# Sending each row only to its two experts: routed blocks of 128 rows in place of all experts on all rows

## The reference

```python
x = layernorm(x + attention(x))            # 16 heads of size 8, softmax over 256 keys
scores = sigmoid(x @ gate_w.T)             # 8 experts
sel = top_k(scores + expert_bias, 2)       # two experts for each token
routed = x[tok] * score                    # the row is scaled, then for expert e of the row:
h = silu(routed @ w1[e].T) * (routed @ w3[e].T)
out_r = (h @ w2[e].T) * score
shared = silu(x @ sw1.T) * (x @ sw3.T) @ sw2.T
x = layernorm(x + shared + sum of the token's two out_r)
```

## Time and profile before

| | us |
|---|---|
| median of three runs | 844.6 |
| lowest and highest | 840.38, 847.2 |
| profiled execution, its time | 847.3 |
| profiled execution, its span | 845.5 |
| attention stage, to the last logits | 469 |
| expert stage | 376 |

### The profile page before, as it was taken

One profiled execution on the slowest core, in us unless ns is written; L12 is line 12 of the kernel. 1 busy time (PEld: TensorE's weight loads), 2 busy tenths in 40 slices (PEclk: granted clock), 3 DMA queues, 4 the chain that ended last, 5 costly groups with the idle time before them and its releaser, 6 DMA issues.

```text
span 845.5 us, 19602 instructions
## 1 busy us (share of the span) xinstructions
PE 762.4 (90%) x6228; PEld 472.6 (56%) x6228; DVE 708.3 (84%) x1430; ACT 579.6 (69%) x1192; POOL 472.3 (56%) x687
## 2 busy tenths in 40 slices
PE   2598999999999999999987889989999999999894
PEld 1234555555555555555545566666666666666662
DVE  5577999999999999999983688888888787887885
ACT  1038999998989999899884566555555655565551
POOL 3336654554555456455212466666766766666664
PEclk9998999999999999999998899999999999999997
DMA  5754767676777677676412633334444544444430
GB/s 156 161 121 105 168 170 168 148 167 169 164 155 178 149 165 167 171 161 144 103 34 68 172 91 91 107 99 104 119 119 110 124 124 124 124 124 121 116 86 26
DMA packets 201682, 109.36 MB, mean 129 GB/s; under 512 B 10496, under 2 KB 201088, under 8 KB 201600
## 3 DMA queue, kind: packets, MB, share of 16 engines
q1 hardware_dynamic: 200048, 105.88, 51.7%
q10 hardware_dynamic: 1552, 2.44, 1.0%
HBM read 73.94 MB, written 33.82 MB: 127 GB/s over the span
## 4 chain that ended last, share of the span: by engine, by line
PE 60%; DVE 11%; POOL 9%; issue 8%; DMA 7%; ACT 2%; SPq 1%; DVEq 1%; POOLq 0%; ACTq 0%
PE bank L732 15%; PE bank L704 10%; PE bank L717 7%; DMA probs<-route_dram 5%; PE bank L739 4%; PE bank L741 3%; PE bank L740 3%; DVE k_stack L1083 3%; POOL place L510 3%; POOL rstd L519 3%; PE bank L814 2%; PE bank L897 2%; PE bank L794 2%; PE bank L834 2%; PE bank L801 2%
## 5 line engine op out<-in xcount | busy, mean ns | idle before, releaser
L1009 DVE TENSOR_REDUCE negmax<-bank 128x2 f32<-128x512 f32 x512 | 320.3, 679 | 31.2 <-PE bank L717 28.7
L558 ACT ACTIVATE probs<-bank 128x512 f32<-128x512 f32 x512 | 291.4, 606 | 44.8 <-PE bank L704 41.1
L717 PE MATMUL bank<-k_stack,q_stack 48*128 48x256 bf16 x1024 | 164.2, 284 | 11.4 <-DMA k_stack<-k_parts_dram 7.3
L704 PE MATMUL bank<-q_stack,k_stack 50*128 50x256 bf16 x1024 | 158.0, 276 | 7.6 <-ACT probs L558 6.1
L739 PE MATMUL bank<-x_hi,hi_w 128*128 128x512 f32 x288 | 137.6, 478 | 14.8 <-DVE k_stack L1083 9.5
L732 PE MATMUL bank<-probs,v_aug 128*32 128x256 f32 x2048 | 139.4, 390 | 0.4 <-ACT attT L569 0.4
L1073 DVE TENSOR_TENSOR k_stack<-bank,probs 128x512 f32<-128x512 f32 x128 | 87.6, 684 | 49.1 <-DMA probs<-route_dram 31.5
L704 PEld LDWEIGHTS bank<-q_stack,k_stack 50*128 50x128 bf16 x1024 | 75.6, 95 | 92.5 <-ACT probs L558 48.5
L741 PE MATMUL bank<-x_lo,hi_w 128*128 128x512 f32 x288 | 114.4, 397 | 0.0
L740 PE MATMUL bank<-x_hi,lo_w 128*128 128x512 f32 x288 | 114.0, 396 | 0.0
L510 POOL TENSOR_TENSOR k_stack<-k_stack,probs 128x512 f32<-128x512 f32 x48 | 62.0, 1293 | 79.1 <-DVE k_stack L1083 71.3
(11 more groups left out here) (116 smaller groups left out, 1338.7 us busy)
## 6 DMA issues: line engine op xcount, KB each, us to landing
probs<-route_dram SPq DMA_DIRECT2D x128, 256.0 KB, 6.0
q_stack<-q_parts_dram SPq DMA_DIRECT2D x64, 192.0 KB, 3.7
k_stack<-k_parts_dram SPq DMA_DIRECT2D x64, 192.0 KB, 4.9
k_parts_dram<-k_parts SPq DMA_DIRECT2D x32, 192.0 KB, 2.2
q_parts_dram<-q_parts SPq DMA_DIRECT2D x32, 192.0 KB, 2.2
xT_sb<-xT SPq DMA_DIRECT2D x32, 128.0 KB, 2.2
k_parts_dram<-k_parts SPq DMA_DIRECT2D x32, 128.0 KB, 2.0
q_parts_dram<-q_parts SPq DMA_DIRECT2D x32, 128.0 KB, 2.2
```

The lines of the kernel that those rows point to most:

```text
L558: nc.scalar.activation(probs[h][:], score_ps[EXP_BANK[h]][:].rearrange("p (j t) -> p j t", j=NT), ACT.Exp).then_inc(exp_done, 1)
L704: mm = pe.matmul(score_ps[EXP_BANK[h]][:, j * T:(j + 1) * T], k_stack[b.ring][first:last, h // 2, j * P:(j + 1) * P], q_stack[b.ring][firs ...
L717: mm = pe.matmul(max_ps[MAX_BANK[h]][:, i * T:(i + 1) * T], q_stack[b.ring][first:last, h // 2, i * P:(i + 1) * P], k_stack[b.ring][first: ...
L1009: nc.vector.tensor_reduce(negmax[b.ring % 2][:, :, column], max_ps[MAX_BANK[h]][:].rearrange("p (i s) -> p i s", i=NT), AX_X, ALU.max, neg ...
```

## The change

The experts no longer see all rows. The 32 batches are cut into five chunks of 6, 8, 8, 6 and 4 batches (12, 16, 16, 12 and 8 tiles). Four slots after a chunk's last batch, DVE ranks its tokens in 26 short steps (`route_steps`, between the reductions of one slot): top two, a running count per expert, with two small matmuls on PE for the counts across partitions, and from that for every token and choice a row number in a DRAM table sorted by expert, each expert's part padded to whole blocks of 128. POOL then sends the rows with **indirect DMAs** (`scatter`), one for each tile and choice, 128 rows of 132 floats each (the row and its score): two or four at each of two places in a slot. Tables are first filled with zeros by 42 DMAs on ACT's queue, two at the start of each of 21 slots (`blanks`).

The expert stage runs over 42 "quads" of four blocks (168 blocks, 128 of them needed if nothing were padded). A quad is loaded by SP, transposed, and each block is multiplied in plain float32 with the weights of its own expert, whose column in SBUF is read into PE's registers from a table (`experts`, a load of four registers per quad). Silu takes the row's score as its scale, and the product takes it again; then a transpose, `down`, and the products go to DRAM. The **shared network** is computed apart, one group of 512 tokens in every two and a half steps, in three pieces in three successive steps. POOL **gathers** the two product rows of each token with 8 indirect DMAs per group, DVE adds them times the score (`combine`) at steps set by COMBINE_AT, and statistics follow a step later. The root of a whole chunk is one POOL instruction (`root`), and ACT does the last layernorm (`norm`). There are 52 steps, 0 to 51; quads end at 41. Gone are the x1T copy, the x1 copy in DRAM, the broadcast weights, the split of the down operand and `weigh`.

```diff
+        SHARED_AT = [1 + (5 * g) // 2 for g in range(GROUPS)]
+        COMBINE_AT = (12, 14, 16, 23, 25, 27, 29, 33, 35, 37, 39, 41, 43, 45, 47, 49)
+        LAST_STEP = COMBINE_AT[-1] + 3
...
+                pool.indirect_dma_start(c.rows_dram, bass.IndirectOffsetOnAxis(ap=slot_column(c, choice, i), axis=0),
+                                        x1_rows[:, c.t0 + i, :], None).then_inc(rows_out[c.c][choice], 16)
...
+            for g in range(GROUPS):
+                gather(g)
+                c = chunk_of_group(g)
+                if c.c and g == c.groups[0]:
+                    root(chunks[c.c - 1])
+            root(chunks[-1])
...
+            def root(c):
+                pool.wait_ge(eps2_set, c.c + 1)
+                tiles = slice(c.t0, c.t0 + c.n)
+                pool.tensor_tensor(rstd2[:, tiles], var_eps2[:, tiles], minus_half[:, 0:c.n], ALU.pow).then_inc(rstd2_set, 1)
...
+            def experts(k):
+                c = chunk_of_quad(k)
+                pe.wait_ge(route_step, steps(c, ROUTE_STEPS))
+                pe.load(registers[k % 2], expert_of[0:1, 4 * k:4 * k + 4])
...
+                for a in range(4):
+                    pe.matmul(up_ps[a // 2][:, a % 2 * 2 * C:a % 2 * 2 * C + 2 * C], xT_q[k % 2][:, a * P:(a + 1) * P],
+                              wall_up[:, bass.ds(first_column(k, a), 2 * C)], start=True, stop=True).then_inc(up_mm, 1)
...
+            def step(k):
+                if k + 1 < QUADS:
+                    rows_turned(k + 1)
+                if 0 < k <= QUADS:
+                    hidden_turned(k - 1)
+                if k < QUADS:
+                    experts(k)
+                    up(k)
+                if 0 < k <= QUADS:
+                    down(k - 1)
...
+                for g in shared_in(k, 2):
+                    shared_down(g)
+                for g in shared_in(k, 1):
+                    shared_up(g)
+                for g in shared_in(k, 0):
+                    shared_turned(g)
...
-                if b.live:
-                    pool.wait_ge(x1T_set, b.count(1, 1))
-                    pool.tensor_copy(x1T[:, bass.ds(b.n * T, T)], x1T_new[:]).then_inc(x1T_kept, 1)
```

More of the change, by code:

```diff
@@ L291, in attention_moe_layer, with normed_in, kept @@
+        def normed_in(k):
+            return [g for g in range(GROUPS) if NORM_AT[g] == k]
+        def kept(c, r):
+            return 16 * len([k for k in range(c.k0 + c.quads) if k % 2 == r])
         block = ctx.enter_context(nc.Block())
@@ L424, in slot, with scatters @@
+            def scatters(s, place):
+                if s == 1 and place == 0:
+                    tables()
+                for c, choice, i in SCATTERS[s, place]:
+                    scatter(c, choice, i)
             def slot(t):
-                if not t.soft.looped and t.soft.c == B:
-                    split_x(0, 0)
                 b = t.neg
@@ new lines, in norm @@
+            def norm(g):
+                act_e.wait_ge(shift2_set, chunk_of_group(g).c + 1)
+                if g >= YO:
+                    act_e.wait_ge(out_sent[g % YO], 16 * (g // YO))
+                for i in range(GT):
+                    t = g * GT + i
+                    nc.scalar.activation(y_out[g % YO][:, i, :], x1_rows[:, t, 0:C], ACT.Identity, bias=shift2[:, t:t + 1],
+                                         scale=rstd2[:, t:t + 1]).then_inc(norm_set, 1)
+                act_e.wait_ge(norm_set, GT * (g + 1))
+                act_e.dma_start(out[g * GT:g * GT + GT, :, :].rearrange("i p c -> p i c"), y_out[g % YO]).then_inc(out_sent[g % YO], 16)
@@ L693, in _ @@
+            rows_to_sbuf(0)
+            for k in range(LAST_STEP):
+                step(k)
         @block.tensor
@@ L928, in _ @@
+            rows_turned(0)
+            for k in range(LAST_STEP):
+                step(k)
         @block.vector
@@ new lines, in shift, with step @@
+            def shift(c):
+                tiles = slice(c.t0, c.t0 + c.n)
+                dve.wait_ge(rstd2_set, c.c + 1)
+                nc.vector.scalar_tensor_tensor(shift2[:, tiles], mv2[:, tiles, 0], -1.0, rstd2[:, tiles], ALU.mult, ALU.mult).then_inc(shift2_set, 1)
+            def step(k):
+                if 0 < k <= QUADS:
+                    hidden_to_sbuf(k - 1)
+                if k < QUADS:
+                    hidden(k)
+                if k == 0:
+                    for h in range(9, H):
+                        route_steps(chunks[-1], h)
+                for g in combined_in(k, 1):
+                    statistics(g)
+                for g in combined_in(k, 0):
+                    combine(g)
+                    c = chunk_of_group(g)
+                    if c.c and g == c.groups[0]:
+                        shift(chunks[c.c - 1])
+                if k == COMBINE_AT[-1] + 2:
+                    shift(chunks[-1])
+                for g in shared_in(k, 2):
+                    base(g)
+                for g in shared_in(k, 1):
+                    shared_hidden(g)
+                for g in shared_in(k, 0):
+                    shared_low(g)
@@ L1164 @@
+            for h in range(9):
+                route_steps(chunks[-1], h)
+            for k in range(LAST_STEP):
+                step(k)
 _OUT_SHAPE = (32, 256, 128)
```

886 lines of the change are left out of this document (474 added, 412 removed).

## The result

The changed kernel took **904.4 us** (903.7 to 906.4, four runs), beside 845.8 for the kernel before on the same chip: a ratio of **1.071** with a 95% interval of 1.066 to 1.076. The forecast was 817, the range 783 to 893. Later the same program, unaltered, took 770, 768 and 911 us on three chips, while the kernel before took 843 to 844 on each. So two answers stand side by side, and both have to be explained: 7% slower where it stalls, 9% faster where it does not. A chip that does not stall is called smooth here. A *send* is a scatter, a *fetch* a gather, and step k is counted from the first weight load of quad k's transposes.

The account below looks back on a forecast made before the run. Prediction: DVE and PE full in attention, PE bounding the experts. 469 + 27.8 + 3 + 2 + 1 - 2.5 + 4 = 504; steps from 508 at 5.9 us, then POOL's gathers: span 818, forecast 817 us, range 783 to 893.

Parts of the forecast that it names:

- the price of an indirect DMA: On POOL's queue, each scatter or gather was estimated at 1.3 us, taken from an instruction over 512 elements.
- POOL as the bound at p = 1.8: Slower rival: p, the time of one indirect DMA, makes POOL the bound; 890 us at 1.8; chance 0.24.
- the rival of the low clock: Expert stage: PE's waits bring its clock to 0.80, T near 7.3 us, time 873; chance 0.06.
- the step of the expert stage, T: Time per quad, set by PE: 5.5 us of work plus 0.4 of exposed register load, 5.9 us.
- Routing: Attention stage: three chunks routed on DVE with nothing hiding them, +27.8 us; the fourth at nothing.
- Scatters in 16 slots: Attention stage: four scatters per slot, 5.2 us, just fit POOL's free time; +3 us for 16 slots.
- The last slots: End of attention stage: 12 early matmuls leave, -2.5 us; 12 scatters ahead of POOL's last root, +4, between 0 and 8.
- 1 for constants and 2 for blanks: Attention stage: three more constants at the start, +1 us net; 42 blank issues on ACT's queue, +2, between nothing and 19.
- the 4 us that I had added behind the logits: Before the first hidden rows, DVE does 16 routing steps of the last chunk, moving the first step from 504 to 508.
- a hidden load: Expert stage: register load fully covered gives T = 5.5, 16 us less; with p = 1.0, 791 us, chance 0.17.
- The end: After step 40, POOL sets the end: third root waits for statistics, then four groups of gathers at 41.6 us; span 818.
- Two of the tests that I had named: Slots without routing over 12.6 us would refute the attention-stage forecast; quads over 6.5 apart would refute the step.

Follow-up runs that it names:

- c2_same: The changed kernel, unaltered, run again on a smooth chip; 767.8 us, 0.912 of the kernel before.
- c1_same: The changed kernel, unaltered, run again in an earlier set on a smooth chip; 769.9 us, 0.911 of the kernel before.
- v1_root_late: The changed kernel with POOL's root of the third chunk moved behind the last group of the fourth chunk's fetches; 762.0 us (0.903) on a smooth chip.
- v3: The changed kernel with the third root late, fetches three to a step, the last 16 sends two to a step; 837.4 us (0.992) on a stalling chip.
- the stretches: Fourteen short loops behind the whole changed kernel, each one engine repeating one operation beside 5 or 8 POOL transfers; first stretch 41.40 us stalling, 39.47 to 40.31 smooth.
- The bench: The changed kernel with the stretches behind it; beside fetches a float32 product took 223 ns on smooth chips.

## Why the prediction was wrong

**The step that failed** is the price of an indirect DMA: the sum charges it to POOL's queue, at 1.3 us, and puts its effect on TensorE at nothing, without a reason. I asked only what POOL had free and what stood behind it on its own queue. No row of the kernel before has such a transfer, so the bounds from below and above covered its length and left out its effect on others. Where it stalls, the runs show that TensorE's counts come late beside a burst, and this costs 134 to 143 us: 904 and 911 against 768 and 770 for the same program. By the traces of the first result and of `c2_same`, the first quad comes 25 us later, steps 0 to 4 take 25 us more and steps 4 to 41 90 more; the part behind step 41 takes 65 us in both. The range had 893 as its end for a different reason, POOL as the bound at p = 1.8. That rival did not happen: p was measured at 0.95 + 0.30 = **1.25 us**, on every chip, against the 1.3 taken. By luck the rival of the low clock names a step of 7.3 us where the first result has 7.4: it has waits bring the clock down and the clock lengthen the step. The clock did fall, to 0.66 from 600 to 640 us, but TensorE issued only 78 matmuls there, so what was missing was mostly work that it was free to do, and not speed.

On a smooth chip the forecast failed as well, to the other side, and there the step of the expert stage, T, was mis-sized. The terms were these (`c2_same`, its profiled execution 764.0, span 762.0, against the 818 forecast for the span):

- *Routing*, forecast +27.8. In the kernel without transfers the logits before and behind a routed slot are 17.8 us apart, and the next slot is longer as well:

```profile
160.88 0.15 DVE L1190 COPY logits<-bank 128x16 f32<-128x16 f32 x1
178.65 0.15 DVE L1190 COPY logits<-bank 128x16 f32<-128x16 f32 x1
192.49 0.15 DVE L1190 COPY logits<-bank 128x16 f32<-128x16 f32 x1
```

  Over 12.30 a slot the two give 5.5 + 1.5, the other chunks 7.8 and 8.8: 23.6 in all. Right in kind, 4 too high.
- *Scatters in 16 slots*, forecast +3: the 25th logits come at 418.6 with sends and at 418.8 without them, so nothing that can be told from how much executions differ (423.9 in `c1_same`). POOL's idle time took them in. Where it stalls the 25th come at 431.0.
- *The last slots*, forecast -2.5 + 4: with up to eight sends in each, ACT's layernorm waited 17.9 us in five slots (longest 8.7) for POOL's root behind them, and the seven last slots took 77.2 us against 63.4 without sends. I had written that a longer scatter ahead of the root "is paid at once", and had priced only the last root. The start, though, was 5.7 us earlier than before (first logits at 98.5 against 104.2), where I had added 1 for constants and 2 for blanks; of the first five slots, all with blanks, four take 12.3 us and one 12.8. Last logits:

```profile
495.83 0.17 DVE L1192 COPY logits<-bank 128x16 f32<-128x16 f32 x1 [8.82 <-PE bank L870]
```

  That is 8 below the forecast 504; in the first result it was 520.40. The first quad's transposes begin at 496.1, with no wait for the 4 us that I had added behind the logits.
- *The step*, forecast T = 5.9, measured 4.94 (steps 3 to 41, 187.9 us). This is the large mis-sized term, 40 us. I had taken durations where PE's rate is the distance between starts: four transposes are 0.43 apart and not 0.59, four down products 0.99 (0.89 in the shared network) and not 1.3. With up at 1.89 and the shared network at 0.43 + 1.39 + 0.89 per group and 1.08 per step, the sum is 0.43 + 0.43 + 1.89 + 0.99 + 1.08 = 4.8. Of the 0.96 us a step, 0.4 is the load that I had left exposed: the register load took 0.33 us and was hidden; the Trainium skill, "DMA: Bandwidth & Descriptors", "Latency and other measured facts", has a floor of 600 ns for it. The trace is below that floor, and the conclusion that I drew from the page and did not use, a hidden load, is the right one. Start, steps and end give 12 + 41 + 3 = 56 us, the whole of 818 - 762.
- *The end*: POOL's, through the third root's wait for statistics, then gathers without a break, as forecast. From step 41 to the end 65 us, forecast 68. ALU.pow took 2.93 us for 16 tiles and 2.30 for 12, not 5.8 and 4.4: it is not proportional to elements. `v1_root_late` shows the mechanism, worth 6 to 8 us.

Two of the tests that I had named fail in the first trace: 9 of the 12 slots with four sends and no routing are 13.2 to 13.8 us long, not under 12.6, and quads are 7.4 apart (steps 4 to 41), not under 6.5. The third, sends over 1.5 us, does not (0.96 us), so the tests found the places and my explanation for them would have been wrong.

**What stays open.** Why some chips hold TensorE's counts back and others do not. The kernel before shows nothing of it, and neither does the length of a gather. A set of runs was of one kind throughout, in up to four rounds over some minutes. One chip's number came up in two sets, once of each kind, so it may be a state that lasts and not the chip. By what path the counts are held, and what in an indirect transfer holds them, is not shown either. That fewer sends in the last slots, or spacing sends in the attention stage (last logits at 522.6 where it stalls, 495.8 where not), would bring v3 further down was not tried.

## What to carry to other kernels

An operation that the profile has never shown has two unknowns, its own length and what it does to the engines beside it; give the second a price, or a rival, of its own. Do not issue many indirect transfers in a row beside a chain that waits for TensorE step by step: put gaps between them (on smooth chips this cost nothing, 768 us). Letting TensorE run ahead by more work may serve as well, by the stretches' 0.1 to 0.4 us against the kernel's 1.0, but no kernel here tried it. Before one believes an edit, the unaltered kernel must run beside it on the same chip: here spacing seemed to give 136 us on one chip and had given nothing, and gave 73 (with the late root) on another.

## What the runs showed that I had not expected

- **Counts of TensorE held back** beside bursts of indirect transfers, on some chips: two counts every 1.4 us, then 18 in 0.72. Not by bytes (rows a quarter as wide: 2.1 us lost for 8, full ones 1.1 to 1.9), nor by rows (32 rows: 3.0).
- **An indirect transfer costs GpSimd nearly the same whatever its size**: 0.95 us for 128 rows, 0.95 for rows a quarter as wide, 0.87 for 32 rows; a plain one of 64 KB takes 0.54 to 0.57.
- **VectorE can shut GpSimd out for as long as it copies in SBUF.** The bench on a smooth chip, VectorE making its last 54 or so copies of 256 columns back to back, one every 0.20 us:

```profile
1086.32 11.66 POOL L385 DMA_INDIRECT q_stack<-y_dram,slots_of  x1 [7.15 <-DVE probs L367]
1098.28 0.94 POOL L385 DMA_INDIRECT q_stack<-y_dram,slots_of  x1 [0.30 <-issue]
```

  One transfer took 11.66 us and ended 0.82 us behind the last copy, so nearly all of its usual 0.94 came after them; the copies kept their pace. It was the same on the stalling chip, and beside products of two SBUF operands a transfer took 12.29 us; beside copies from PSUM, 0.94. The Trainium skill, "SBUF — State Buffer", section "Who interferes with whom", says that whoever issues first gets the shared pair "for the whole instruction", and that the other blocks. I read this as a lock that ends with each instruction; by that GpSimd should have got in after 0.20 us. Here hardly any of its work was done between copies.
